# Context and x loaded with 64 consecutive rows per partition, strips transposed at a step of 64 words, l worked out group by group

## The chip, the cores and the metric

One core of a Trainium2 chip runs the whole kernel: TensorE (PE), VectorE (DVE), ScalarE (ACT), GpSimd (POOL), and SyncE (SP), which here only issues DMAs. The metric is the device time of one execution in microseconds. Times are given as the median of several executions; one execution was also profiled.

## The reference

The kernel computes one graph attention layer over 8192 nodes with a residual and a layer norm. `adj` is 8192 x 8192 float32 of zeros and ones (268 MB), `context` 8192 x 512, `x` 8192 x 256.

```python
in_fts = context @ W_common.T
left   = in_fts @ w_left  + b_left      # l, one number per row of adj
right  = in_fts @ w_right + b_right     # r, one number per column of adj
logits = left[:, None] + right[None, :]
logits = where(logits >= 0, logits, 0.2 * logits)
logits = where(adj <= 0, -inf, logits)
h      = relu(softmax(logits, axis=-1) @ x)
out    = layernorm(x + h, axis=-1, eps=1e-5)
```

## The kernel before

The weight vectors are folded first: `v = W_common.T @ w` for both sides, replicated over all partitions in PSUM (L267), so that l and r are dot products of context rows with `v`.

**Setup.** SP loads context in 8 chunks of 2 MB, each as four DMAs of 32 partitions (L200). Partition `32q + p` takes the rows `2048q + 32j + p`: a row per piece, 2 KB. The chunks go through four buffers that lie in X, so chunk 4 and later wait for earlier dot products. DVE forms all 64 r and 24 of the l dot products (L418); the other 40 l go through a product on POOL (L249) and a sum on ACT (L305). Then come extremes of r, exponentials, and the tables: `tab` in PSUM holds for each partition quadrant the packed word of every one of its 2048 columns (L472), `arow` the word of every row (16 small copies, L476). x (8.4 MB) is loaded after that in 16 DMAs of 1 KB pieces (L212). ACT takes square sums of x (64 of L321), DVE a scale `Fx`, then ACT writes the 64 high parts of x (L326) and DVE the 64 low parts (L510) as float16 into X, which are the moving side of all later products.

**Main loop.** adj is taken in 256 strips `n` of 32 rows, 1 MB each; a strip lies in one of four buffers as 128 partitions x 2048 words, quadrant q holding columns 2048q to 2048q + 2047. Four strips make a group `g` of 128 rows; there are 64 groups. Per strip: four DMAs (L175, waiting for the transpose of the strip four earlier), ACT turns 0/1 into a mask (L351), DVE picks the word of each edge by max and min against `tab` and `arow[:, n]` (L518, `masked(n)`), and DVE transposes 32 x 32 blocks into T (L562, `transposed(n)`). T has two halves, so the first transpose of group g waits for the products of group g - 2. Per group PE runs 192 matmuls of 257 columns (L291, L292 and L295 for each of 64 blocks), 12288 in all. What remains of a group (reciprocal, quotient, residual, norm, store) is small and trails two groups behind.

**Order.** All engines run programs written out by hand, with semaphores. The block that is transposed for product `jb` is the set of columns `2048q + 32 jb + i`, 32 consecutive words of the strip in each quadrant, which has to match the row of x that partition `32q + i` holds in X:

```python
nc.vector.transpose(T[:, o, :, k * B:(k + 1) * B],
                    strip[:, b, :].rearrange("p (j i) -> p j i", i=B)).then_inc(s_t, 1)
```

A second path for a wide range of exponents (`general_steps`) exists in both kernels and is not taken with these inputs.

Of the kernel before, what the change touches and what calls it, by code (L numbers as in the profile page):

```python
# [11 lines left out]
AX = mybir.AxisListType  # L12

# [9 lines left out]
def build(nc, x, adj, ctx_in, w_common, w_left, b_left, w_right, b_right, out):  # L23
# [16 lines left out]
    NX = 4  # L40
    XC = JB // NX
    HB = JB // 2
    OWN = [j for j in range(JB) if j % 8 in (0, 3, 6)]
# [13 lines left out]
    with stack:  # L57
# [14 lines left out]
        LR = sb("LR", [P, 2, JB])  # L72
        E = sb("E", [P, 2, JB])
        Et = sb("Et", [P, 2, JB])
        word = sb("word", [P, 2, JB])
        gen = sb("gen", [P, 2, JB])
        F = sb("F", [P, JB])
        Fx = sb("Fx", [P, JB])
        SS = sb("SS", [P, JB])
        wcol = sb("wcol", [P, 2, HID // P])  # L80
        bias = sb("bias", [P, 2])
        small = sb("small", [P, 64])
        y = xs2[:, 0:NY, :]
        xrow = xs2[:, NY:NY + 2, :]

# [4 lines left out]
        word16 = word[:, :, :].rearrange("p c j -> p (c j)").bitcast(F16).rearrange("p (c j e) -> p c j e", c=2, e=2)  # L90
        cstage = [Xflat[:, s * CT * CIN:(s + 1) * CT * CIN].rearrange("p (t k) -> p t k", k=CIN) for s in range(4)]
        xs1 = T[:, 1, :, :].rearrange("p j m -> p (j m)").rearrange("p (j d) -> p j d", d=D)
        W = strip[:, 3, 0:2 * CIN].rearrange("p (h k) -> p h k", h=2)
        wrep = strip[:, 3, 2 * CIN:2 * CIN + 4 * P].rearrange("p (c h m) -> p c h m", c=2, h=2)
        vl = strip[:, 2, 0:CIN]
        prod = strip[:, 2, CIN:3 * CIN].rearrange("p (b k) -> p b k", b=2)

        def xrows(j):
            return xs1[:, j, :] if j < HB else xs2[:, j - HB, :]
# [10 lines left out]
        mxc, diag = small[0:3, 28:29], small[0:3, 29:32]  # L110

# [4 lines left out]
        pt = stack.enter_context(nc.psum_tensor("pt", [P, 512], F32))  # L116
        tab = stack.enter_context(nc.psum_tensor("tab", [P, NQ], F32))
# [5 lines left out]
        s_ctx = [sem(f"context_in{s}") for s in range(4)]  # L123
# [3 lines left out]
        s_vl = sem("v_left_copied")  # L127
        s_prod = sem("product_ready")
        s_sum = sem("product_summed")
        s_dot = sem("dots_done")  # L130
        s_lr = sem("left_right_ready")
# [14 lines left out]
        s_xl = sem("x_low_ready")  # L146
        s_one_col = sem("ones_column_steps")
# [23 lines left out]
        def _(sp):  # L171
# [14 lines left out]

            sp.dma_start(W, w_common.rearrange("(p h) k -> p h k", p=P)).then_inc(s_w, 16)
            for c, v in enumerate((w_right, w_left)):
                sp.dma_start(wcol[:, c, :], v.rearrange("(p h) -> p h", p=P)).then_inc(s_w, 16)
            for c, v in enumerate((b_right, b_left)):  # L190
                sp.dma_start(bias[:, c:c + 1], v.broadcast_to([P, 1])).then_inc(s_w, 16)
            for c in range(NCH):
                if c >= 4:
                    end = (c - 3) * CT
                    own = sum(j < end for j in OWN)
                    sp.wait_ge(s_dot, end + own)
                    sp.wait_ge(s_prod, end - own)
# [4 lines left out]
            for n in range(2):  # L202
                load_strip(n)
            sp.wait_ge(s_sum, JB - len(OWN))
            sp.wait_ge(s_v, 1)
            for n in range(2, NB):
                load_strip(n)
            for c in range(NX):
                dst = (xs1, xs2)[c // (NX // 2)][:, c % (NX // 2) * XC:(c % (NX // 2) + 1) * XC, :]
                for q in (0, 2, 1, 3):  # L210
                    r0 = q * NQ + c * XC * B
                    sp.dma_start(dst[q * B:(q + 1) * B, :, :],  # L212
                                 x[r0:r0 + XC * B, :].rearrange("(j p) d -> p j d", p=B)).then_inc(s_x[c], 16)
            sp.wait_ge(s_xh, JB)
            sp.wait_ge(s_xl, JB)
            for g in range(2):
                load_xrow(g)
            for n in range(NS):
                g, k = divmod(n, SG)
                if n + NB < NS:  # L220
                    sp.wait_ge(s_t, n + 1)
                    load_strip(n + NB)
                if k == 2 and g >= 2:
                    load_xrow(g)
                if k == 2 and g >= 3:
                    store(g - 3)
# [6 lines left out]
        def _(pool):  # L233
# [6 lines left out]
            pool.wait_ge(s_vl, 1)  # L240
            m = 0
            for c in range(NCH):
                pool.wait_ge(s_ctx[c % 4], 64 * (c // 4 + 1))
                for t in range(CT):
                    if c * CT + t in OWN:
                        continue
                    if m >= 2:
                        pool.wait_ge(s_sum, m - 1)
                    nc.gpsimd.tensor_tensor(prod[:, m % 2, :], cstage[c % 4][:, t, :], vl, ALU.mult).then_inc(s_prod, 1)  # L249
                    m += 1  # L250
# [11 lines left out]
        def _(pe):  # L262
            pe.wait_ge(s_w, 80)
            pe.wait_ge(s_wrep, 1)
            for c in range(2):
# [16 lines left out]
            for g in range(NG):  # L282
                o = g % 2
                pe.wait_ge(s_t, (g + 1) * SG)
                if g >= 2:
                    pe.wait_ge(s_y, g - 1)
# [354 lines left out]
```

## Time and profile before

| | |
|---|---|
| median of 3 runs | 1564.39 us (1547.11 to 1564.72) |
| the profiled execution | 1557.17 us |
| its span | 1555.3 us |
| PE busy / DVE busy / ACT busy | 89% / 82% / 44% |
| mean granted clock of PE | 0.947 |

The span is the stretch that the trace covers, and the execution's own time is 1.9 us longer. PE's matmuls overlap one another in the record (a mean of 273 ns each, while a new one starts every 111 ns), so its busy time tells when it works, not how well.

### The profile page before, as it was taken

The numbers are of one execution on the slowest core, as the hardware profiler recorded it, in microseconds if no ns is written. First come the engines' busy times: TensorE is split into PE (matmuls) and PEld (weight loads), VectorE is DVE, ScalarE is ACT, GpSimd is POOL, SyncE is SP. The second block draws the span as 40 slices with busy tenths as digits, with TensorE's granted clock in tenths as the row PEclk, the third lists the DMA queues.
The fourth block names the chain that finished last, engine by engine and source line by source line (L and its number), as shares of the span: only waits on it lengthen the run. The fifth ranks groups of instructions, "written<-read, shape, count | busy, mean of one in ns | idle before, by whom it ended". The sixth has DMA issues, their size and how long they took to land.

```text
span 1555.3 us, 28279 instructions
## 1 busy us (share of the span) xinstructions
PE 1379.9 (89%) x12302; PEld 1199.8 (77%) x12302; DVE 1269.4 (82%) x1000; ACT 685.9 (44%) x852; POOL 110.2 (7%) x240
## 2 busy tenths in 40 slices
PE   1002379999999999999999999999999999999998
PEld 0002268888888888888888888888888888888887
DVE  4883698898888988888988888888889888889881
ACT  2458544444444444444444444444444444444440
POOL 4710000000000000000000000000000000000000
PEclk7555789999999999999999999999999999999999
DMA  9994598888888888888888888888888888888870
GB/s 212 270 200 87 139 220 208 221 206 207 211 208 216 213 205 211 206 207 224 203 210 210 208 210 220 205 207 211 209 218 211 205 212 208 207 223 204 208 177 12
DMA packets 85584, 312.82 MB, mean 201 GB/s; under 512 B 19792, under 2 KB 44368, under 8 KB 52688
## 3 DMA queue, kind: packets, MB, share of 16 engines
q1 hardware_dynamic: 85456, 310.98, 81.2%
q8 instruction: 96, 1.57, 0.5%
q14 instruction: 32, 0.26, 0.1%
HBM read 302.52 MB, written 8.39 MB: 200 GB/s over the span
## 4 chain that ended last, share of the span: by engine, by line
PE 87%; DMA 5%; SPq 4%; DVE 3%; ACT 1%; POOL 0%; issue 0%; POOLq 0%; DVEq 0%
PE ps L295 29%; PE ps L291 29%; PE ps L292 29%; DMA X<-in_L_gnn_context_dram 3%; SPq L212 2%; DVE X L510 2%; DMA xs<-in_x_dram 1%; SPq L200 1%; DMA strip<-in_adj_dram 1%; ACT pt L321 1%; SPq L175 1%; DVE gw L418 0%; DVE strip L518 0%; DVE T L562 0%; POOL strip L249 0%
## 5 line engine op out<-in xcount | busy, mean ns | idle before, releaser
L291 PE MATMUL ps<-X,T 128*128 128x257 f16 x4096 | 1117.3, 273 | 34.5 <-DVE T L562 32.8
L295 PE MATMUL ps<-X,T 128*128 128x257 f16 x4096 | 1125.2, 275 | 0.0
L292 PE MATMUL ps<-X,T 128*128 128x257 f16 x4096 | 1114.8, 272 | 0.0
L562 DVE STREAM_TRANSPOSE T<-strip 128x2048 f32<-128x2048 f32 x256 | 589.4, 2303 | 174.8 <-PE ps L295 174.8
L351 ACT ACTIVATE strip<-strip 128x2048 f32<-128x2048 f32 x256 | 488.8, 1910 | 413.7 <-DMA strip<-in_adj_dram 413.4
L518 DVE SCALAR_TENSOR_TENSOR strip<-tab,arow,strip 128x2048 f32<-128x2048 f32 x256 | 595.1, 2325 | 17.3 <-ACT strip L351 17.0
L291 PEld LDWEIGHTS ps<-X,T 128*128 128x128 f16 x4096 | 403.5, 99 | 85.0 <-DVE T L562 33.0
L292 PEld LDWEIGHTS ps<-X,T 128*128 128x128 f16 x4096 | 399.0, 97 | 61.3
L295 PEld LDWEIGHTS ps<-X,T 128*128 128x128 f16 x4096 | 397.2, 97 | 63.2 <-DVE X L510 7.5
L332 ACT ACTIVATE xs<-ps,small 128x256 f32<-128x256 f32 x64 | 30.4, 475 | 219.9 <-DVE small L567 219.9
L255 POOL TENSOR_SCALAR small<-small 128x1 f32<-128x1 f32 x64 | 12.3, 192 | 1398.9 <-ACT pt L340 1398.9
L336 ACT ACTIVATE small<-small 128x1 f32<-128x1 f32 x64 | 13.0, 203 | 156.2 <-DVE xs L572 156.2
L418 DVE SCALAR_TENSOR_TENSOR gw<-X,ps 128x512 f32<-128x512 f32 x88 | 54.2, 683 | 20.7 <-DMA X<-in_L_gnn_context_dram 20.7
L273 PE MATMUL pt<-ident,small 128*2 128x128 f32 x1 | 0.4, 372 | 69.0 <-DVE small L433 69.0
L273 PEld LDWEIGHTS pt<-ident,small 128*2 128x2 f32 x1 | 0.1, 80 | 70.1 <-issue 70.1
L249 POOL TENSOR_TENSOR strip<-X,strip 128x512 f32<-128x512 f32 x40 | 49.6, 1273 | 32.5 <-DMA X<-in_L_gnn_context_dram 32.5
L277 PE MATMUL pt<-ident,small 128*1 128x128 f32 x1 | 0.4, 372 | 55.5 <-DVE small L489 55.5
L277 PEld LDWEIGHTS pt<-ident,small 128*1 128x1 f32 x1 | 0.1, 79 | 55.6 <-DVE small L489 55.6
L305 ACT ACTIVATE strip<-strip 128x512 f32<-128x512 f32 x40 | 25.2, 630 | 38.8 <-POOL strip L249 38.8
L345 ACT ACTIVATE xs<-xs,small 128x256 f32<-128x256 f32 x64 | 37.5, 586 | 3.6 <-POOL small L259 3.6
L257 POOL TENSOR_TENSOR small<-small 128x1 f32<-128x1 f32 x64 | 35.2, 551 | 5.3
L340 ACT ACTIVATE pt<-xs,small 128x256 f32<-128x256 f32 x64 | 30.6, 478 | 2.1
(71 smaller groups left out, 198.3 us busy)
## 6 DMA issues: line engine op xcount, KB each, us to landing
strip<-in_adj_dram SPq DMA_DIRECT2D x1024, 256.0 KB, 4.6
X<-in_L_gnn_context_dram SPq DMA_DIRECT2D x32, 512.0 KB, 16.9
xs<-in_x_dram SPq DMA_DIRECT2D x64, 128.0 KB, 5.0
out_dram<-xs SPq DMA_DIRECT2D x64, 128.0 KB, 4.9
T<-in_x_dram SPq DMA_DIRECT2D x8, 512.0 KB, 13.9
xs<-in_x_dram SPq DMA_DIRECT2D x8, 512.0 KB, 14.1
strip<-in_L_gnn_W_common_dram SPq DMA_DIRECT2D x1, 512.0 KB, 3.6
wcol<-in_L_gnn_w_right_dram SPq DMA_DIRECT2D x1, 1.0 KB, 3.3
```

The lines of the kernel that those rows point to most:

```text
L212: sp.dma_start(dst[q * B:(q + 1) * B, :, :], x[r0:r0 + XC * B, :].rearrange("(j p) d -> p j d", p=B)).then_inc(s_x[c], 16)
L249: nc.gpsimd.tensor_tensor(prod[:, m % 2, :], cstage[c % 4][:, t, :], vl, ALU.mult).then_inc(s_prod, 1)
L257: nc.gpsimd.tensor_tensor(st(5, o), st(4, o), power, ALU.pow).then_inc(s_rstd, 1)
L291: nc.tensor.matmul(ps[o][:, 0:D + 1], hi, X16[:, jb, 0:D + 1], start=(jb == 0), stop=False)
L292: nc.tensor.matmul(ps[o][:, 0:D + 1], lo, X16[:, jb, 0:D + 1], start=False, stop=False)
L295: m = nc.tensor.matmul(ps[o][:, 0:D + 1], hi, X16[:, jb, D + 2:2 * D + 3], start=False, stop=(jb == JB - 1))
L345: nc.scalar.activation(y[:, o, :], y[:, o, :], ACT.Identity, scale=st(5, o), bias=st(6, o)).then_inc(s_out, 1)
L351: nc.scalar.activation(s, s, ACT.Relu, scale=KEEP).then_inc(s_m, 1)
L418: nc.vector.scalar_tensor_tensor(out=gw[:, junk * CIN:(junk + 1) * CIN], in0=cstage[c % 4][:, t, :], scalar=1.0, in1=ps[side][:, 0:CIN], o ...
L510: nc.vector.scalar_tensor_tensor(out=X16[:, j, D + 2:2 * D + 2], in0=xrows(j), scalar=Fx[:, j:j + 1], in1=X16[:, j, 0:D], op0=ALU.mult, op ...
L518: nc.vector.scalar_tensor_tensor(out=s, in0=tab[:, :], scalar=arow[:, n:n + 1], in1=s, op0=ALU.max, op1=ALU.min).then_inc(s_p, 1)
L562: nc.vector.transpose(T[:, o, :, k * B:(k + 1) * B], strip[:, b, :].rearrange("p (j i) -> p j i", i=B)).then_inc(s_t, 1)
```

## The change

Context and x are laid out so that partition p holds rows 64p to 64p + 63. Each context chunk is then one DMA over 128 partitions in pieces of 16 KB, with a home of its own (T and X), and waits for nothing; x follows in four such DMAs. Word `64i + j` of a strip's quadrant now belongs with partition `32q + i`, block j, so the transposes read the strip at a step of 64 words, and `tab` is written in that order.

In this layout DVE gets r from the 64 dot products, but not l in the order of the rows of adj. For l, 512 context rows (1 MB) are loaded once more for each four groups (`load_left_rows`), 16.8 MB over the kernel; DVE forms four dot products (`left_dot`), spreads them by strip (`left_by_strip`), PE carries the result to all quadrants (`spread_left`), and DVE and ACT turn it into 16 words of `arow` (`left_step`, `left_exponentials`), all interleaved with the strips of the four groups before. POOL's and ACT's share of the l products is gone. The first four strips are loaded right behind x; square sums cover two rows at once (32 instructions) and run before the first masks; the 64 high parts stand between the first masks; POOL forms 24 of the low parts and DVE 40; in group 0 PE runs all products with high parts first and the 64 with low parts after them.

```diff
-                for q in (0, 2, 1, 3):
-                    rows = ctx_in[q * NQ + c * CT * B:q * NQ + (c + 1) * CT * B, :]
-                    sp.dma_start(cstage[c % 4][q * B:(q + 1) * B, :, :],
-                                 rows.rearrange("(t p) k -> p t k", p=B)).then_inc(s_ctx[c % 4], 16)
+            def load_left_rows(b):
+                rows = ctx_in[b * LB * P:(b + 1) * LB * P, :].rearrange("(g p) k -> p g k", p=P)
+                sp.dma_start(lctx0 if b == 0 else lctx, rows).then_inc(s_lc, 16)
+            def load_context(c):
+                sp.dma_start(cstage[c], ctx_in.rearrange("(p j) k -> p j k", p=P)[:, c * CT:(c + 1) * CT, :]).then_inc(
+                    s_ctx[c], 16)
...
+                if n % LW == 12 and n // LW + 2 < NLB:
+                    b = n // LW + 2
+                    sp.wait_ge(s_ld, LB * b)
+                    load_left_rows(b)
...
+            for j in range(0, NPL, XB):
+                rows = xrows(j, XB)
+                pool.wait_ge(s_xh, j + XB)
+                nc.gpsimd.tensor_tensor(rows, rows,
+                                        Fx[:, j:j + XB].rearrange("p (j c) -> p j c", c=1).broadcast_to([P, XB, D]),
+                                        ALU.mult).then_inc(s_xf, 1)
+                pool.wait_ge(s_xf, j // XB + 1)
+                nc.gpsimd.tensor_tensor(X16[:, j:j + XB, D + 2:2 * D + 2], rows, X16[:, j:j + XB, 0:D],
+                                        ALU.subtract).then_inc(s_xp, XB)
...
+            def spread_left(b):
+                pe.wait_ge(s_lm, b + 1)
+                if b >= 2:
+                    pe.wait_ge(s_la, 3 * (b - 1))
+                nc.tensor.matmul(pt[:, 0:LW], R[:, :, :].rearrange("p q i -> p (q i)"),
+                                 L[:, :, :].rearrange("p g s -> p (g s)"), start=True, stop=True).then_inc(s_lb, 1)
...
+                if g % LB == 1 and g // LB + 1 < NLB:
+                    spread_left(g // LB + 1)
...
+            for j in range(HB):
+                if 2 * j % XC == 0:
+                    act.wait_ge(s_x[2 * j // XC], 16)
+                if j >= 1:
+                    act.wait_ge(s_ss, j)
+                nc.scalar.activation(ps[1][:, 0:2 * D], xrows(2 * j, 2).rearrange("p j d -> p (j d)"), ACT.Square,
+                                     accum_out=SS[:, j:j + 1]).then_inc(s_ss, 1)
...
-            nc.vector.transpose(tab[:, :].rearrange("p (j c) -> p j c", c=B),
+            nc.vector.transpose(tab[:, :].rearrange("p (c j) -> p j c", c=B),
...
                 nc.vector.transpose(T[:, o, :, k * B:(k + 1) * B],
-                                    strip[:, b, :].rearrange("p (j i) -> p j i", i=B)).then_inc(s_t, 1)
+                                    strip[:, b, :].rearrange("p (i j) -> p j i", i=B)).then_inc(s_t, 1)
```

The new helper that DVE runs between strips (b is the block of four groups ahead, k the strip within the present one):

```python
def left_step(b, k):
    if 7 <= k < 7 + LB:
        q = k - 7
        if q == 0:
            dve.wait_ge(s_lc, (b + 1) * 16)
        dve.wait_ge(s_ld, b * LB + q - 1)
        left_dot(b, q, lctx, ljunk[:, q % 2, :])
    if k == 11:
        left_by_strip(b)
    if k == 13:
        ...   # three instructions on 16 columns
    if k == 14:
        ...   # waits for ACT's exponentials, then five on 16 columns
```

DVE's program in the main loop, before: the end of a group, and the first strips of the next. L518 is the mask step, L562 the transpose, L567 and L572 finish an older group.

```order
L518 SCALAR_TENSOR_TENSOR strip<-tab,arow,strip 128x2048 [waits mask_or_exponentials_ready]
L562 STREAM_TRANSPOSE T<-strip 128x64x32 [waits words_masked,products_done]
L567 RECIPROCAL small<-ps 128x1 [waits products_done]
L518 SCALAR_TENSOR_TENSOR strip<-tab,arow,strip 128x2048 [waits mask_or_exponentials_ready]
L562 STREAM_TRANSPOSE T<-strip 128x64x32 [waits words_masked]
L572 SCALAR_TENSOR_TENSOR xs,small<-xs,small 128x256 [waits xrow_in0,quotient_ready]
```

The same place in the changed kernel, at the last group of a block (L622 is the mask step, L666 the transpose).

```order
L666 STREAM_TRANSPOSE T<-strip 128x64x32 [waits words_masked]
L599 TENSOR_SCALAR E<-pt,small 128x16 [waits left_on_all_quadrants]
L600 TENSOR_SCALAR gen<-pt,small 128x16
L602 TENSOR_SCALAR E<-E,small 128x16 [waits left_exponent_steps]
L676 SCALAR_TENSOR_TENSOR xs,small<-xs,small 128x256 [waits xrow_in1,quotient_ready]
L622 SCALAR_TENSOR_TENSOR strip<-tab,arow,strip 128x2048 [waits mask_or_exponentials_ready]
L666 STREAM_TRANSPOSE T<-strip 128x64x32 [waits words_masked]
L605 TENSOR_SCALAR Et<-E 128x16 [waits left_exponentials_ready]
L608 TENSOR_TENSOR E<-E,Et 128x16 [waits left_word_steps]
L609 TENSOR_SCALAR word<-Et 128x16
L611 TENSOR_SCALAR word<-E 128x16 [waits left_word_steps]
L614 SCALAR_TENSOR_TENSOR arow<-word,small,gen 128x16 [waits left_word_steps]
```

Per four groups DVE gains four dot products, one spreading step and these eight small ones, with one new wait for PE and one for ACT.

ACT's program in the setup, before, from the end of the l sums on (L351 is the mask, L321 a square sum, L326 a high part).

```order
L309 ACTIVATE E<-E 128x128 [waits exponents_ready]
L311 ACTIVATE F<-F 128x64 [waits exponents_ready]
L351 ACTIVATE strip<-strip 128x2048 [waits adj_in0]
L321 ACTIVATE pt,SS<-T 128x256 [waits x_in0]
L321 ACTIVATE pt,SS<-xs 128x256 [waits x_square_sums,x_in2]
L326 ACTIVATE X<-T,Fx 128x256 [waits x_factors_ready]
L326 ACTIVATE X<-xs,Fx 128x256 x32
```

And in the changed kernel (L400 is the mask, L364 a square sum over two rows, L371 a high part).

```order
L356 ACTIVATE E<-E 128x80 [waits exponents_ready]
L358 ACTIVATE F<-F 128x64 [waits exponents_ready]
L364 ACTIVATE ps,SS<-xs 128x512 [waits x_in0]
L364 ACTIVATE ps,SS<-T 128x512 [waits x_square_sums,x_in2]
L400 ACTIVATE strip<-strip 128x2048 [waits adj_in0]
L371 ACTIVATE X<-xs,Fx 128x256 [waits x_factors_ready] x10
L400 ACTIVATE strip<-strip 128x2048 [waits adj_in1]
L371 ACTIVATE X<-xs,Fx 128x256 [waits x_factors_ready] x10
```

The square sums now stand ahead of the first mask, and the high parts are spread among the first four masks.

## Rows read from the trace of the kernel before

**Rows 1.** Page: busy time and share of the span.

```profile
PE 1379.9 (89%) x12302; PEld 1199.8 (77%) x12302; DVE 1269.4 (82%) x1000; ACT 685.9 (44%) x852; POOL 110.2 (7%) x240
```

**Rows 2.** Windows: busy us of each engine, granted clock, DMA share, GB/s.

```profile
120.00:140.00 20.00, 0.00 (x0) 0.00 (x0) 0.00 (x0) 17.32 (x70) 0.00 (x0) 0.50 0.68 134
180.00:200.00 20.00, 0.00 (x0) 0.00 (x0) 16.72 (x8) 8.20 (x5) 0.00 (x0) 0.50 0.96 229
300.00:600.00 300.00, 300.00 (x2702) 263.28 (x2701) 258.52 (x156) 131.44 (x127) 13.07 (x42) 1.00 0.85 210
```

**Rows 3.** Waits: engine and line, awaited, us in total, times, longest.

```profile
ACT strip L351 <- DMA strip<-in_adj_dram: 413.4, 194, 8.6
DVE T L562 <- PE ps L295: 174.8, 61, 3.0
```

**Rows 4.** Timeline of DVE in mid-loop: start, us, instruction, idle before.

```profile
717.23 2.31 DVE L562 STREAM_TRANSPOSE T<-strip 128x2048 f32<-128x2048 f32 x1 [2.96 <-PE ps L295]
719.47 0.13 DVE L567 RECIPROCAL small<-ps 128x1 f32<-128x1 f32 x1
719.52 2.32 DVE L518 SCALAR_TENSOR_TENSOR strip<-tab,arow,strip 128x2048 f32<-128x2048 f32 x1
721.76 2.30 DVE L562 STREAM_TRANSPOSE T<-strip 128x2048 f32<-128x2048 f32 x1
...
738.57 2.31 DVE L562 STREAM_TRANSPOSE T<-strip 128x2048 f32<-128x2048 f32 x1 [2.96 <-PE ps L295]
```

**Rows 5.** Timeline of the setup: start, us, instruction.

```profile
84.04 0.25 DVE L426 TENSOR_SCALAR LR<-LR,bias 128x64 f32<-128x64 f32 x1
...
96.21 2.35 DVE L518 SCALAR_TENSOR_TENSOR strip<-tab,arow,strip 128x2048 f32<-128x2048 f32 x1 [0.26 <-issue]
...
144.35 12.89 ACT L326 ACTIVATE X<-T,Fx 128x256 f16<-128x256 f32 x32 [2.59 <-DVE Fx L504]
...
203.73 0.39 PE L291 MATMUL ps<-X,T 128*128 128x257 f16 x1 [32.85 <-DVE T L562]
```

**Rows 6.** Chain that ended last, in the setup: start, us, what.

```profile
26.94 3.14 DVE gw L418 x10
...
83.50 0.73 ACT strip L305 x2
...
140.72 0.52 ACT pt L321 x2
...
142.81 0.59 PE pt L279 x2
...
144.97 25.59 DVE X L510 x64
...
176.92 11.32 DMA strip<-in_adj_dram
```

**Rows 7.** Windows of the DMA in the setup, columns as in rows 2.

```profile
2.00:6.00 4.00, 0.00 (x0) 0.00 (x0) 0.00 (x0) 0.00 (x0) 0.00 (x0) 1.00 0.49 155
...
66.00:70.00 4.00, 0.00 (x0) 0.00 (x0) 3.21 (x11) 1.61 (x6) 2.62 (x3) 0.50 1.05 302
...
180.00:184.00 4.00, 0.00 (x0) 0.00 (x0) 2.35 (x1) 1.46 (x2) 0.00 (x0) 0.50 1.00 231
```

**Rows 8.** Groups by line and shape: busy us, mean ns, idle before.

```profile
L249 POOL TENSOR_TENSOR strip<-X,strip 128x512 f32<-128x512 f32 x40 | 49.6, 1273 | 32.5 <-DMA X<-in_L_gnn_context_dram 32.5
...
L476 DVE COPY arow<-word 32x64 f32<-32x64 f32 x16 | 2.9, 184 | 0.2
L472 DVE STREAM_TRANSPOSE tab<-word 128x2048 f32<-128x2048 f32 x1 | 2.3, 2327 | 0.0
...
L482 DVE SCALAR_TENSOR_TENSOR X<-F,X 128x64 f16<-128x64 f32 x1 | 0.4, 448 | 0.0
L480 DVE TENSOR_SCALAR X<-F 128x64 f16<-128x64 f32 x1 | 0.3, 320 | 0.0
...
L465 DVE TENSOR_SCALAR word<-Et 128x128 f16<-128x128 f32 x1 | 0.2, 234 | 0.0
```

More of the change, by code:

```diff
@@ L40, in build @@
     NX = 4
+    LB = 4
+    NLB = NG // LB
+    LW = LB * SG
+    NPL = 24
     XC = JB // NX
     HB = JB // 2
-    OWN = [j for j in range(JB) if j % 8 in (0, 3, 6)]
     WSCALE = 2.0 ** 10
@@ L218, in _ @@
+            for c in range(NX):
+                if c == NX // 2:
+                    sp.wait_ge(s_dot, 2 * CT)
+                sp.dma_start(xrows(c * XC, XC), x.rearrange("(p j) d -> p j d", p=P)[:, c * XC:(c + 1) * XC, :]).then_inc(
+                    s_x[c], 16)
+            sp.wait_ge(s_v, 2)
+            for n in range(NB):
+                load_strip(n)
             for n in range(NS):
@@ L312, in _, with high_part @@
             act.wait_ge(s_set, 4)
             general = act.value_load(flag.bitcast(I32)[0:1, 0:1])
[L315 to L323 removed]
+            def high_part(j):
@@ L324, in high_parts, with left_exponentials @@
                 act.wait_ge(s_Fx, 1)
-                for j in range(JB):
-                    nc.scalar.activation(X16[:, j, 0:D], xrows(j), ACT.Copy, scale=Fx[:, j:j + 1]).then_inc(s_xh, 1)
+                nc.scalar.activation(X16[:, j, 0:D], xrows(j), ACT.Copy, scale=Fx[:, j:j + 1]).then_inc(s_xh, 1)
+            def left_exponentials(b):
+                act.wait_ge(s_la, b * 3)
+                nc.scalar.activation(E[:, lw], E[:, lw], ACT.Exp, scale=1.0 - SLOPE).then_inc(s_le, 1)
             def quotient(g, o, turn):
@@ L370, in general_steps @@
                         exponentials((it * NY + u) * SG + k, k % NB)
+                        if more and u * SG + k == 13:
+                            left_exponentials(it + 1)
             with act.If(general == 0):
@@ L374, in _ @@
                     keep(n)
-                square_sums()
-                high_parts()
+                    for j in range(n * 10, n * 10 + 10):
+                        high_part(j)
+                for j in range(NB * 10, JB):
+                    high_part(j)
                 for n in range(NB, NS):
@@ L388, in _ @@
             with act.Else():
-                square_sums()
-                high_parts()
+                for j in range(JB):
+                    high_part(j)
                 general_steps(0)
                 general_steps(1)
-                with act.Fori(2, NG // NY) as it:
+                with act.Fori(2, NG // NY - 1) as it:
                     general_steps(it)
+                general_steps(NG // NY - 1, more=False)
             for g in range(NG - 2, NG):
@@ L579, in finish, with general_steps @@
                     residual(g, o, turn)
-            def general_steps(it):
+            def general_steps(it, more=True):
                 for u in range(NY):
```

335 lines of the change are left out of this document (188 added, 147 removed).

## Prediction

> **What bounds the kernel now.** I read the page's busy shares first, then the windows, then the waits. PE is busy for 89% of the span and nothing else comes near it except DVE with 82% [rows 1], so the question is where PE is bound by itself and where it waits. The windows answer it: from 300 us on every 300 us hold 2702 matmuls without a gap at the full clock [rows 2], one each 111 ns. 192 of them make a group, 21.3 us, and the timeline of DVE shows the same step, 717.23 to 738.57 [rows 4]. The waits show what is left on the others: DVE waits for PE 61 times, 174.8 us in total, 2.87 us per group; ACT waits for adj DMAs 413.4 us [rows 3]. So in the loop PE sets the time, DVE has 2.87 of 21.3 us to spare, and DMA is busy for 85% [rows 2]. Only what happens before PE's unbroken run can be saved. That run begins at 203.73 us with group 1 [rows 5], and 1351.6 us later the span ends, which is 63 groups plus a short tail. The first 204 us are a chain: DMA of context, then of x, ACT's square sums, high and low parts, and then the wait for strips that could not be fetched before (11.32 us of DMA at 176.92) [rows 6].
>
> **The setup.** I rebuild the chain of the changed kernel from these rows.
> Context: 0.5 MB of weights, 16.8 MB and the first 1 MB for l, with no wait between. The rate isn't shown for such loads in bulk. The nearest rows are 155 GB/s at a DMA share of 0.49 while the weights came in (the one large load over 128 partitions), 316 GB/s if scaled to a full share; 302 for context at its fastest; 231 for strips [rows 7]. I take 302: last chunk at 2 + 61 = 63 us. DVE needs 0.63 us per dot product (10 records in 3.14 us) [rows 6], 8 after the last chunk: 68 us, against 84.04 now [rows 5].
> Tables: 12.2 us from there to the first mask now [rows 5]; the 16 copies (2.9 us) [rows 8] become one. They end near 78 and nobody waits: ACT needs only the exponents, some 4 us after the dot products.
> x: 8.4 MB more at 302 GB/s, 91 us. Square sums over 512 words: 0.73 us for the two records of such an ACT step, 0.52 us for 256 words [rows 6]; 32 of them take 24 us instead of 35, from 72 to 96, and the last chunk of x leaves 6 us after 91. Both give 97. The scale takes 2.6 us, the idle time in front of L326 [rows 5]: 99.
> Strips 0 to 3 land between 94 and 105, just behind x, and no longer hold anything up. The second four are fetched during what follows, which removes the 11.32 us.
> Then ACT: 30 high parts at 0.403 us (12.89 us for 32) [rows 5] and three masks at 1.9 between them bring the mask of strip 3 to 117. DVE's mask step and transpose follow (4.5 us, from the starts 719.52 and 721.76 and the next step) [rows 4]: 121.5. 40 low parts at 0.40 (25.59 us for 64) [rows 6]: 137.5. Eight steps for strips 4 to 7 at 2.23: PE begins group 1 at 155. POOL's 12 instructions on 1024 words, twice 1273 ns each [rows 8], end near 130 and are covered by DVE's low parts. That cover is 8 us deep; beyond it each us counts only for group 0, which has another 18 us.
> Sum: 203.7 - 155 = 48 us earlier.
> Bounds: at 231 GB/s everything moves back by 27 us (21 us gained). With a DMA faster than DVE, 68 dot products of 0.63 us set the pace and the start is at 143 (61 us gained).
> POOL may also get in the way of DVE. In this trace POOL never works beside a DVE instruction with two SBUF inputs; the low parts are such. The overlap is 10 us, so the price lies between 0 and 10 us; I take 0. The Trainium skill, page "SBUF — State Buffer", section "Who interferes with whom", calls the port pair of the two an exclusive lock; by it the price would be near the 10 us, and no row here shows it.
>
> **The loop.** DVE's additions per four groups: four dot products (2.5 us), nine small instructions that I price like L465, 0.23 us [rows 8], so 4.6 us, 1.15 per group. DVE goes from 18.5 to 19.6 us in 21.3: hidden, and 1.7 us per group, 0.43 per transpose, are left as cover.
> PE's additions: 15 products of a 128 x 128 float32 weight with 16 columns. The nearest is L279, 0.59 us for two records [rows 6]; I take 0.5 each, 7 us in all, on the path; bounds 0 and 9. They wait for a DVE step that comes before the last transposes of a later group, about 3 us before PE gets there.
> DMA: 15 more MB in 1344 us raise the share from 0.85 to about 0.9. Each MB takes 4.5 us at 231 GB/s in front of one strip. A strip's path (issue, landing, mask) has a few us to spare, and DVE's lateness is made up from the 1.7 us per group. I take 0; if every one were paid, 63 us.
> ACT: one more exponential per four groups, ACT is half idle. DVE waits for it at strip 14 of 16, behind ACT's mask of strip 16; that is at hand about when DVE comes. Queued behind this wait is DVE's next mask step. 0, up to 1.7 us per group without effect.
>
> **The transposes.** 252 of them stand in the loop, 2.30 us each for 2048 words at a step of one [rows 4]. Now they read at a step of 64 words. No row shows a wide read step alone. Two rows write float16 at a step of 1032 bytes: L480 takes 320 ns for 64 elements where L465 takes 234 for 128, so a wide write is dear. L482 reads one stream and writes at that step, 448 ns, 128 ns more than L480, or 2.0 ns per element; but it is another operation, with two inputs, and reads from the place where it writes [rows 8]. By it a transpose could cost up to 4.1 us more. For a transpose itself there is one other reading pattern: L472 reads each word 32 times in succession and takes 2327 ns, against 2303 for contiguous words. Fetching 32 times fewer words makes it no faster: the pace is one element per cycle of DVE, not the fetch, and the output is written in runs of 32 words in either kernel. I take 0, the value of the nearest row in kind, and keep 4.1 us as the other end.
> The Trainium skill says otherwise: "Advanced Engine Details and Errata", section "Memory Cachelines", has SBUF lines of 16 bytes and wants at least two hits on a line to absorb the latency; a step of 256 bytes hits each line once. It gives no figure; the rival below has it as a doubling. The step from L480 to L482 speaks for it, L472 is silent on it.
>
> **Sum.** 1557.2 (the profiled execution, 1.9 above its span) - 48 + 7 = 1516 us. The median of the runs is 7 us above the profiled one; I forecast 1520 us. The bounds of rate, POOL and PE give 1500 to 1550.
>
> **Rivals.**
> (A) The strided reads cost DVE two cycles per element, 2.13 us more per transpose. DVE then needs 19.6 + 8.5 = 28.1 us per group, more than PE: 63 x 28.1 from about 140, plus PE's last group and the tail (27 us), 1940 us. It decides from 2.9 us per transpose: 0.43 are covered, and each 0.1 above costs 25 us, so the 41 us are gone at 0.16 more. For it: L482, and that DVE has little to spare. Against it: L472 and L562 alike. Chance 0.18. At the far end (4.1 us more) it would be 2.4 ms; that is included.
> (B) A part of that, a transpose of 2.9 to 3.4 us: 1545 to 1680 us. Chance 0.09.
> (C) The gain is given back: context at the rate of the strips (27 us), POOL in DVE's way (10), late strips behind the l rows (some of the 63), so that PE shows gaps once in four groups. 1535 to 1580. For it: the DMA share of 0.85 and ACT's waits on strips. Against: DVE's spare time. Chance 0.13.
> (D) Loads over 128 partitions run so fast that DVE sets the pace of the setup: 1490 to 1505. The row with 316 GB/s at a scaled share speaks for it. Chance 0.05.
>
> **How the numbers follow.** The forecast has 0.55. A difference under 2%, 1533 to 1596 us, is about what a measurement can't tell from none (the three runs spread over 1.1%). Faster by over 2%: 0.50 of the forecast and D, 0.55. Within 2%: 0.05 of the forecast, 0.12 of C and 0.01 of B, 0.18. Slower: A, 0.08 of B and 0.01 of C, 0.27. The range has to hold 8 in 10: it leaves out A and the lowest end of D, and takes in B: 1495 to 1680. The forecast's own range is 1500 to 1550.
>
> **What would show it.** In the profile of the changed kernel: L666 at 2.3 us (A: 4.4), with waits on PE of some 1.7 us per group; PE's unbroken run from about 155 us, 2702 matmuls per 300 us less those for l; the last context chunk by 63 us; square sums done by 97; 40 low parts on DVE at 0.40 us beside POOL's. I am wrong if DVE shows no wait for PE in the loop and PE waits for L666 in every group (A, B), if PE's gaps come every fourth group (C), or if x lands later than 100 us.

## The result, and the profile after

The changed kernel takes 1728.9 us (median of 4; 1728.4 to 1730.5) against 1563.7 us before: a ratio of 1.106, 95% interval 1.104 to 1.109. The forecast was 1520 us, range 1495 to 1680: a gain was forecast and a loss came.

The page of the changed kernel, the rows that answer to [rows 1], and its costliest groups on DVE (columns as in [rows 8]):

```profile
PE 1435.1 (83%) x12334; PEld 1225.6 (71%) x12334; DVE 1659.2 (96%) x1181; ACT 645.9 (37%) x722; POOL 84.3 (5%) x212
...
L666 DVE STREAM_TRANSPOSE T<-strip 128x2048 f32<-128x2048 f32 x256 | 951.1, 3716 | 0.0
...
L622 DVE SCALAR_TENSOR_TENSOR strip<-tab,arow,strip 128x2048 f32<-128x2048 f32 x256 | 599.0, 2340 | 4.3 <-ACT strip L400 3.7
```

DVE has gone from 82% to 96% and PE from 89% to 83%. Mask steps cost what they did; a transpose has gone from 2.3 to 3.7 us, and the idle time in front of it from 174.8 us [rows 3] to zero. DVE is the bound. The windows say the same as a count: 300 us used to hold 2702 matmuls [rows 2], now 2330. PE's granted clock is 0.95 in this window, against 1.00 before, now that PE has gaps; DVE is busy in 299.36 of the 300 us, so the clock of PE sets nothing here.

```profile
300.00:600.00 300.00, 272.48 (x2330) 232.39 (x2329) 299.36 (x184) 112.35 (x112) 11.15 (x36) 0.95 0.77 191
```

The waits have turned round. In [rows 3] DVE waited for PE; now PE waits for DVE, at the first product of a group (L336) and at the small product that spreads l (L307). The lines give the us in total, how often, and the longest:

```profile
ACT strip L400 <- DMA strip<-in_adj_dram: 503.8, 147, 19.5
...
PE ps L336 <- DVE T L666: 134.0, 49, 28.3
...
PE pt L307 <- DVE L L476: 92.6, 16, 20.7
```

DVE's timeline in mid-loop gives the step of four groups, from one L605 to the next (start, us, instruction):

```profile
702.01 0.13 DVE L605 TENSOR_SCALAR Et<-E 128x16 int32<-128x16 int32 x1
...
702.86 2.35 DVE L622 SCALAR_TENSOR_TENSOR strip<-tab,arow,strip 128x2048 f32<-128x2048 f32 x1
705.13 3.68 DVE L666 STREAM_TRANSPOSE T<-strip 128x2048 f32<-128x2048 f32 x1
708.72 2.32 DVE L622 SCALAR_TENSOR_TENSOR strip<-tab,arow,strip 128x2048 f32<-128x2048 f32 x1
...
801.58 0.13 DVE L605 TENSOR_SCALAR Et<-E 128x16 int32<-128x16 int32 x1
```

99.57 us for four groups, 24.9 us per group, where PE alone sets 21.3 [rows 4]. No idle time stands in front of any of these rows. The mask step of strip 4 starts at 132.67 us; 63 groups of 24.9 us from there, and 26 us for PE's last group and the tail, make 1727, the span.

The setup did become short. DMA moved 431 GB/s from 20 to 40 us and 389 from 40 to 60, more than any row before showed; DVE's dot products waited twice at the start, 7.5 us in all, and then followed one another; the last ended at 58.3 us, and PE began group 1 at 158.24 us instead of 203.73 [rows 5].

```profile
20.00:40.00 20.00, 0.58 (x2) 0.50 (x2) 17.74 (x54) 0.00 (x0) 0.00 (x0) 0.50 1.01 431
...
158.24 0.40 PE L336 MATMUL ps<-X,T 128*128 128x257 f16 x1 [18.55 <-DVE T L666]
```

### The profile page after: what moved, and what is told of

Read it like the earlier page. It is cut to its first block, busy times and chain, and to the rows that moved or that the text cites. A ratio compares the mean times of both kernels' runs of the same rounds, so it can differ in the third digit from the quotient of the medians.

```text
span 1727.0 us, 28390 instructions
## 1 busy us (share of the span) xinstructions
PE 1435.1 (83%) x12334; PEld 1225.6 (71%) x12334; DVE 1659.2 (96%) x1181; ACT 645.9 (37%) x722; POOL 84.3 (5%) x212
## 4 chain that ended last, share of the span: by engine, by line
DVE 71%; issue 24%; ACT 2%; PE 1%; DMA 1%; SPq 0%; POOL 0%; POOLq 0%; ACTq 0%; DVEq 0%
DVE strip L622 33%; DVE T L666 30%; DVE xs L471 2%; DVE tab L488 2%; DVE xs L676 1%; ACT ps L364 1%; DMA T<-in_L_gnn_context_dram 1%; DVE X L583 1%; PE ps L336 0%; PE ps L339 0%; PE ps L337 0%; DVE small L671 0%; ACT X L371 0%; DVE arow L614 0%; DVE gen L600 0%
## 5 line engine op out<-in xcount | busy, mean ns | idle before, releaser
L336 PE MATMUL ps<-X,T 128*128 128x257 f16 x4096 | 1135.0, 278 | 134.0 <-DVE T L666 134.0
L337 PE MATMUL ps<-X,T 128*128 128x257 f16 x4096 | 1132.1, 277 | 0.0
L339 PE MATMUL ps<-X,T 128*128 128x257 f16 x4032 | 1125.7, 279 | 0.0
L666 DVE STREAM_TRANSPOSE T<-strip 128x2048 f32<-128x2048 f32 x256 | 951.1, 3716 | 0.0
L400 ACT ACTIVATE strip<-strip 128x2048 f32<-128x2048 f32 x256 | 488.2, 1908 | 505.5 <-DMA strip<-in_adj_dram 503.8
L622 DVE SCALAR_TENSOR_TENSOR strip<-tab,arow,strip 128x2048 f32<-128x2048 f32 x256 | 599.0, 2340 | 4.3 <-ACT strip L400 3.7
L336 PEld LDWEIGHTS ps<-X,T 128*128 128x128 f16 x4096 | 413.0, 101 | 204.8 <-DVE T L666 119.2
L337 PEld LDWEIGHTS ps<-X,T 128*128 128x128 f16 x4096 | 406.1, 99 | 66.9
L339 PEld LDWEIGHTS ps<-X,T 128*128 128x128 f16 x4032 | 398.1, 99 | 61.9
L307 PE MATMUL pt<-L,R 128*128 128x16 f32 x32 | 9.1, 365 | 92.6 <-DVE L L476 92.6
L307 PEld LDWEIGHTS pt<-L,R 128*128 128x128 f32 x32 | 7.5, 289 | 97.6 <-DVE L L476 76.1
L471 DVE SCALAR_TENSOR_TENSOR xs<-xs,vl 128x512 f32<-128x512 f32 x60 | 39.1, 652 | 0.0
L394 ACT ACTIVATE xs<-xs,small 128x256 f32<-128x256 f32 x64 | 37.5, 586 | 3.6 <-POOL small L292 3.6
L389 ACT ACTIVATE xs<-xs,small 128x256 f32<-128x256 f32 x64 | 32.6, 509 | 2.1
L676 DVE SCALAR_TENSOR_TENSOR xs<-xs,small 128x256 f32<-128x256 f32 x64 | 30.0, 469 | 1.3 <-ACT xs L381 1.1
L671 DVE RECIPROCAL small<-ps 128x1 f32<-128x1 f32 x64 | 9.2, 144 | 20.5 <-PE ps L339 20.5
L488 DVE SCALAR_TENSOR_TENSOR tab<-T,ps 128x512 f32<-128x512 f32 x32 | 20.9, 726 | 7.5 <-DMA T<-in_L_gnn_context_dram 7.5
```

Of the source, the lines that this page charges most:

```text
L336: nc.tensor.matmul(ps[o][:, 0:D + 1], hi, X16[:, jb, 0:D + 1], start=(jb == 0), stop=False)
L337: nc.tensor.matmul(ps[o][:, 0:D + 1], lo, X16[:, jb, 0:D + 1], start=False, stop=False)
L339: m = nc.tensor.matmul(ps[o][:, 0:D + 1], hi, X16[:, jb, D + 2:2 * D + 3], start=False, stop=(jb == JB - 1))
L389: nc.scalar.activation(junk_row, y[:, o, :], ACT.Square, bias=st(2, o), accum_out=st(3, o)).then_inc(s_var, 1)
L394: nc.scalar.activation(y[:, o, :], y[:, o, :], ACT.Identity, scale=st(5, o), bias=st(6, o)).then_inc(s_out, 1)
L400: nc.scalar.activation(s, s, ACT.Relu, scale=KEEP).then_inc(s_m, 1)
```

## The experiments

Two theories stood at first. **S**: the step of 64 words alone makes DVE the bound. **L**: the work for l, put into the loop, is a large part of it. Later runs ask what the step costs and where, what made the setup short, and whether the gain can be had without the price. Where an edit leaves columns or rows matched otherwise than in the reference, the expectation says so; of such a run only the time and the trace are used.

### One line back: contiguous reads

```diff
-                                    strip[:, b, :].rearrange("p (i j) -> p j i", i=B)).then_inc(s_t, 1)
+                                    strip[:, b, :].rearrange("p (j i) -> p j i", i=B)).then_inc(s_t, 1)
```

> The changed kernel with one line back: the transposes read 32 consecutive words again (the table and the layout stay, so columns are matched wrongly and the output is not the reference's). Theory S, the step of 64 words alone makes the loop slow: transposes 2.3 us instead of 3.7, DVE below PE again (19.6 us of 21.3 per group), PE without gaps, 1512 us. Theory L, the l steps in the loop (DVE's dot products, PE's waits for them) are a large part: transposes 2.3 us, but gaps of PE stay and the time is above 1560 us.

Measured: 1508.5 us (1507.7 to 1508.7), 0.965 of the kernel before (0.9635 to 0.9667). S holds, L falls: with all of the l work in the loop PE runs without gaps. A window of this run, its transposes, and then DVE's largest waits:

```profile
300.00:600.00 300.00, 300.00 (x2705) 263.37 (x2703) 271.84 (x215) 131.34 (x129) 13.08 (x42) 1.00 0.89 221
```

```profile
L666 DVE STREAM_TRANSPOSE T<-strip 128x2048 f32<-128x2048 f32 x256 | 589.1, 2302 | 79.7 <-PE ps L339 79.7
```

```profile
DVE T L666 <- PE ps L339: 79.7, 47, 3.0
DVE strip L622 <- ACT strip L400: 46.4, 23, 3.7
```

DVE is left with 126.1 us of waiting, 2.0 us per group. That is the cover of this loop: the work that DVE can take on before PE has to wait for it. The one line costs 220 us.

### The same line in the kernel before

```diff
-                                    strip[:, b, :].rearrange("p (j i) -> p j i", i=B)).then_inc(s_t, 1)
+                                    strip[:, b, :].rearrange("p (i j) -> p j i", i=B)).then_inc(s_t, 1)
```

> The kernel before with one line changed: the transposes read at a step of 64 words (columns are matched wrongly, the output is not the reference's). Nothing of the l steps is in it. Theory S: DVE needs 18.5 + 4 x 1.4 = 24.2 us per group, 63 groups from about 188 us and PE's last group: 1740 us. Theory L: the transposes alone cost less than DVE has spare, under 1600 us.

Measured: 1723.9 us (1721.5 to 1724.6), a ratio of 1.103. Its transposes take 3707 ns, and 2402 matmuls stand in the 300 us from 300 on.

```profile
L562 DVE STREAM_TRANSPOSE T<-strip 128x2048 f32<-128x2048 f32 x256 | 948.7, 3707 | 0.0
```

So the step is sufficient by itself, in either setup.

### How much of it is covered

```diff
+                view = "p (i j) -> p j i" if k in (0,) else "p (j i) -> p j i"
                 nc.vector.transpose(T[:, o, :, k * B:(k + 1) * B],
-                                    strip[:, b, :].rearrange("p (j i) -> p j i", i=B)).then_inc(s_t, 1)
+                                    strip[:, b, :].rearrange(view, i=B)).then_inc(s_t, 1)
```

(the second run has `k in (0, 2)`; both start from the run with contiguous reads)

> As the run with contiguous reads (1508.5 us), but the first of the four transposes of each group reads at a step of 64 words (output not the reference's). If DVE's spare time is a true cover, one such transpose (1.43 us) fits into what DVE has left in that run (waits of 79.7 + 46.4 us, 2.0 us per group): at most 1515 us. If any delay of DVE reaches PE, 63 x 1.43 = 90 us more, 1598 us.

> As before, with the first and third transpose of each group at a step of 64 words: 2.86 us per group against 2.0 of cover, so 0.86 x 63 = 54 us more than 1508.5: 1562 us by the cover; 1688 us if nothing is covered.

Measured: 1510.3 us and 1573.5 us. The transposes of the two runs:

```profile
L667 DVE STREAM_TRANSPOSE T<-strip 128x2048 f32<-128x2048 f32 x256 | 683.3, 2670 | 8.5 <-PE ps L339 8.5
```

```profile
L667 DVE STREAM_TRANSPOSE T<-strip 128x2048 f32<-128x2048 f32 x256 | 776.7, 3035 | 0.0
```

One wide transpose per group, 94 us of DVE's work in all (683.3 against 589.1), costs 2 us; two cost 65 us, four cost 220. That is a cover with an edge near 2 us per group. The second came out 11 us above the expectation. Some 5 of them are the price, 1.47 us per wide transpose here (776.7 against 589.1, 128 of them wide) in place of 1.43. For the rest, DVE still waits 15.9 us for ACT's masks there, so it may be that not all of its spare time can be used; that was not tried by itself.

### Steps by themselves

A kernel with no other work, run once: DVE instructions on 2048 words, four of each, one after the other.

> No part of the computation: 2048-word transposes, masks and copies on DVE by themselves, each four times, at steps of 1, 2, 4, 8, 16, 32, 64 words and in rows padded to 65, 68, 72 and 96 words, to and from PSUM, and a wide write step; ACT copies at steps 1 and 64. If the cost is one of 16-byte lines, steps 1 and 2 take 2.3 us and 4 and above 3.7. If it is a bank conflict, step 64 costs more than 65 or 68. If it belongs to reading and writing SBUF at once, a step-64 transpose into PSUM takes 2.3 us. If every strided read of DVE pays, the mask and the copy at a step of 64 take 1.4 us more too.

DVE's timeline; the lines are, in order, transposes at steps of 1, 2, 4, 64 and 65 words, at 64 words into PSUM, at 64 words out of PSUM, at 64 words on the side that is written, and the mask operation contiguous and with a read at 64 words:

```profile
15.40 9.35 DVE L61 STREAM_TRANSPOSE dst<-src 128x2048 f32<-128x2048 f32 x4
24.78 9.35 DVE L64 STREAM_TRANSPOSE dst<-src 128x2048 f32<-128x2048 f32 x4
34.17 15.35 DVE L67 STREAM_TRANSPOSE dst<-src 128x2048 f32<-128x2048 f32 x4
...
94.24 14.60 DVE L79 STREAM_TRANSPOSE dst<-src 128x2048 f32<-128x2048 f32 x4
108.88 15.40 DVE L85 STREAM_TRANSPOSE dst<-src 128x2048 f32<-128x2048 f32 x4
...
184.38 14.55 DVE L101 STREAM_TRANSPOSE pm<-src 128x2048 f32<-128x2048 f32 x4
198.97 9.37 DVE L105 STREAM_TRANSPOSE dst<-pm 128x2048 f32<-128x2048 f32 x4
208.37 14.62 DVE L108 STREAM_TRANSPOSE wide<-src 128x2048 f32<-128x2048 f32 x4
223.02 9.27 DVE L112 SCALAR_TENSOR_TENSOR flat<-pm,src 128x2048 f32<-128x2048 f32 x4
232.32 14.53 DVE L116 SCALAR_TENSOR_TENSOR flat<-pm,src 128x2048 f32<-128x2048 f32 x4
```

A step of two words is free. From four words on the price is nearly the same, 1.3 to 1.5 us per 2048 words, at 4, 8, 16, 32, 64, 65, 68, 72 and 96. Padding rows to 65 words does not help, so it is not a conflict that the power of two makes. It belongs to SBUF on either side and to the mask operation as well; a wide read out of PSUM costs nothing. A plain copy of 2048 words goes from 1.25 to 1.92 us. ACT pays more: 1910 ns contiguous, 3782 at a step of 64.

### Finer steps, and the two small rows

> No part of the computation: more steps on DVE and ACT, each four times. If the limit is 16 bytes, transposes at a step of 3 words (12 bytes) take as long per block as at 1, at 4 words longer; masks on 1024 float16 words pay at a step of 8 elements (16 bytes), not at 4; float32 at 4 words, not at 2 or 3. The two small rows that the prediction read (64 elements, step 1032 bytes): near and far reads and writes apart; if wide reads cost 0.7 ns per element, the far read adds 45 ns, and the rest of the 128 ns belongs to reading and writing there at once or to the other operation. ACT: steps of 2, 4 and a wide write.

This kernel too was run once. 1024 float16 words in the mask operation take 1225 ns at a step of 4 elements and some 1.96 us at 8; float32 words 1224 ns at steps of 1 and 2, some 1.96 us at 4. Transposes of 1536 words take 2.23 us at a step of 3 words and 2.91 at 4; the contiguous rate of 2312 ns for 2048 would give 1.73. So it goes by bytes: free at 8, part of the price at 12, all of it at 16. ACT takes 1910 ns for 2048 words at a step of 1, 2.05 us at 2, 3.85 at 4, and 3.76 with the step of 64 words on the side that it writes. The small instructions on 64 elements (groups by line and shape):

```profile
L124 DVE SCALAR_TENSOR_TENSOR xw<-src,flat 128x64 f16<-128x64 f32 x4 | 1.8, 440 | 0.1
L128 DVE SCALAR_TENSOR_TENSOR xw<-src,xw 128x64 f16<-128x64 f32 x4 | 1.8, 440 | 0.1
...
L113 DVE TENSOR_SCALAR xw<-src 128x64 f16<-128x64 f32 x4 | 1.2, 311 | 0.1
...
L120 DVE SCALAR_TENSOR_TENSOR flat<-src,xw 128x64 f16<-128x64 f32 x4 | 1.1, 278 | 0.1
L116 DVE SCALAR_TENSOR_TENSOR flat<-src,flat 128x64 f16<-128x64 f32 x4 | 0.9, 224 | 0.1
L110 DVE TENSOR_SCALAR flat<-src 128x64 f16<-128x64 f32 x4 | 0.8, 196 | 0.1
```

L116 reads and writes near, L120 reads at a step of 1032 bytes, L124 writes at it, L128 does both. L110 and L113 are the operation with one input, near and with the wide write. The wide read alone adds 54 ns, 0.84 ns per element. With the wide write the read adds nothing: 440 and 440.

### What made the setup short

> The changed kernel with the layout of the kernel before (context in pieces of 2 KB and x in pieces of 1 KB, four DMAs of 32 partitions each, but still with homes of their own and no waits; contiguous transposes, table in the old order). The whole computation is done. Theory S: faster than both kernels, as far as the setup's gain holds without the 64-row layout: with 230 to 300 GB/s in the setup 1520 to 1540 us, against 1512 with the long pieces. If the layout itself is what makes the setup short: 1550 us or more.

Its edit puts back the four DMAs of 32 partitions, contiguous transposes and the old table order:

```diff
-                sp.dma_start(cstage[c], ctx_in.rearrange("(p j) k -> p j k", p=P)[:, c * CT:(c + 1) * CT, :]).then_inc(
-                    s_ctx[c], 16)
+                for q in (0, 2, 1, 3):
+                    rows = ctx_in[q * NQ + c * CT * B:q * NQ + (c + 1) * CT * B, :]
+                    sp.dma_start(cstage[c][q * B:(q + 1) * B, :, :],
+                                 rows.rearrange("(t p) k -> p t k", p=B)).then_inc(s_ctx[c], 16)
```

Measured: 1549.0 us (1548.0 to 1552.2), 0.991 (0.989 to 0.993). The loop is whole again (2705 matmuls in 300 us), but only 14 of the 55 us remain: homes of their own, no waits and the rest of the new setup are worth little when the loads run at 222 to 236 GB/s, and PE begins group 1 at 195.21 us. The missing 40 us are the rate, as the next run shows. It is not a fixed number: the profiled execution of the kernel before, with such DMAs too, moved 234, 255 and 280 GB/s in the three windows from 20 to 80 us, and the kernel before with the one line changed (the second run above), whose setup is the same, 229, 228 and 231. Why was not tried.

> As the run with contiguous reads, but context and x come in single DMAs over 128 partitions with one row per piece (2 KB and 1 KB) in place of 16 KB pieces (rows in another order, output not the reference's). It tells apart what makes the setup's loads fast. If it is the 128 partitions of one DMA, the setup stays as short: 1508 to 1515 us. If it is the length of the pieces, the loads run at 220 to 240 GB/s as in the run with the old layout: 1545 to 1552 us.

```diff
-                sp.dma_start(cstage[c], ctx_in.rearrange("(p j) k -> p j k", p=P)[:, c * CT:(c + 1) * CT, :]).then_inc(
+                sp.dma_start(cstage[c], ctx_in.rearrange("(j p) k -> p j k", p=P)[:, c * CT:(c + 1) * CT, :]).then_inc(
```

(x likewise, and the transposes are contiguous.) Measured: 1509.2 us (1508.6 to 1510.3). The pieces are as short as in the kernel before, and the time is that of the long ones. One window of each of these two runs, first with 32 partitions, then with 128:

```profile
20.00:40.00 20.00, 0.00 (x0) 0.00 (x0) 8.35 (x27) 0.00 (x0) 0.00 (x0) 0.50 1.07 236
```

```profile
20.00:40.00 20.00, 0.58 (x2) 0.50 (x2) 17.03 (x52) 0.00 (x0) 0.00 (x0) 0.50 1.05 387
```

Both have the DMA share full (1.07 and 1.05). The reach of one DMA over the partitions makes the rate, not the 64 consecutive rows. One thing changed along with the reach: a DMA is 2 MB in the fast run and 512 KB in the slow one. Two traces speak against the size. In the run with the old layout one DMA still reaches over 128 partitions, the first 1 MB for l in pieces of 2 KB; by its place in the queue it runs from about 24 to 27 us, and these are the windows there:

```profile
22.00:24.00 2.00, 0.00 (x0) 0.00 (x0) 0.00 (x0) 0.00 (x0) 0.00 (x0) 0.50 1.06 205
24.00:26.00 2.00, 0.00 (x0) 0.00 (x0) 1.54 (x5) 0.00 (x0) 0.00 (x0) 0.50 1.03 374
26.00:28.00 2.00, 0.00 (x0) 0.00 (x0) 2.00 (x7) 0.00 (x0) 0.00 (x0) 0.50 1.10 235
```

And 512 KB DMAs over 128 partitions (the run after the next) moved 105 GB/s at a DMA share of 0.26, which is 404 if scaled to a full share. A 512 KB DMA over 128 partitions that keeps all engines busy was not run.

### Versions that do the whole computation

**Two rows per piece** (a step of two words in the transposes, still 32 partitions per DMA):

> Whole computation. Layout with two consecutive rows of context and x per piece (4 KB and 2 KB), so that transposes read at a step of two words, which cost nothing in the steps run (9.35 us for four, as for a step of one). Transposes 2.3 us, loop as in the run with contiguous reads; the setup gains as far as 4 KB pieces go faster than 2 KB ones: 1525 to 1548 us.

```diff
-                                 rows.rearrange("(t p) k -> p t k", p=B)).then_inc(s_ctx[c], 16)
+                                 rows.rearrange("(t p u) k -> p t u k", p=B, u=2)).then_inc(s_ctx[c], 16)
...
-                                    strip[:, b, :].rearrange("p (j i) -> p j i", i=B)).then_inc(s_t, 1)
+                                    strip[:, b, :].rearrange("p (j i u) -> p j u i", i=B, u=2)).then_inc(s_t, 1)
```

Measured: 1550.3 us (1548.7 to 1551.5), transposes 2305 ns. The step is free in the kernel as well, and pieces of twice the length bring nothing (235, 224 and 223 GB/s from 20 to 80 us).

**The same, each DMA over all 128 partitions** as four quadrants of 32:

> Whole computation. The layout with two consecutive rows per piece (transposes at a step of two words, which cost nothing), but every DMA of context and x covers all 128 partitions: 32 DMAs of 512 KB and 32 of 256 KB in place of 32 and 16 over 32 partitions. If the reach over 128 partitions makes the setup's loads fast, as the run with short pieces says, DMA runs at 370 GB/s or more and the time is 1507 to 1520 us, faster than every version that does the whole computation. If only the large single DMAs were fast (their number, SP's issue of some 0.5 us each), 1540 us or more.

```diff
...
+                    sp.dma_start(cstage[c][:, u:u + 2, :].rearrange("p u k -> p (u k)"),
+                                 ctx_in.rearrange("(q j p u) k -> q p j (u k)", q=Q, p=B, u=2)[:, :, t, :]).then_inc(
+                                     s_ctx[c], 16)
```

Measured: 1690.7 us (1690.1 to 1691.3). A clear miss, of the setup alone: the loop has 2706 matmuls in 300 us. A window of the setup:

```profile
100.00:140.00 40.00, 0.00 (x0) 0.00 (x0) 10.59 (x32) 0.00 (x0) 0.00 (x0) 0.50 0.26 105
```

A DMA share of 0.26 is four of sixteen engines, and the outermost dimension of the source is now the four quadrants. The Trainium skill, page "DMA: Bandwidth & Descriptors", section "Rules for kernel authors", says that an outermost dimension of c < 16 confines the whole DMA to at most c engines; the trace agrees, with 105 GB/s.

**Two queues.** The two-row version with 32 partitions per DMA; SP issues quadrants 0 and 1, ACT quadrants 2 and 3.

> Whole computation. The layout with two consecutive rows per piece, in DMAs over 32 partitions that spread over all DMA engines, as in the run that gave 1550 us; but ACT, which has nothing to do in the setup, issues those of quadrants 2 and 3 while SP issues 0 and 1. If the 220 to 236 GB/s come from one DMA of 32 partitions at a time being served, with two queues two quadrants are written at once and the rate is 380 GB/s or more: 1508 to 1520 us. If a DMA over 32 partitions is slow whatever runs beside it, 1545 to 1555 us.

```diff
+            for c in range(NCH):
+                for q in (2, 3):
+                    rows = ctx_in[q * NQ + c * CT * B:q * NQ + (c + 1) * CT * B, :]
+                    act.dma_start(cstage[c][q * B:(q + 1) * B, :, :].rearrange("p (t u) k -> p t u k", u=2),
+                                  rows.rearrange("(t p u) k -> p t u k", p=B, u=2)).then_inc(s_ctx[c], 16)
```

Measured: 1529.4 us (1529.1 to 1530.6), 0.978 (0.976 to 0.979). Between the two expectations: the rate is 268, 304 and 306 GB/s in the three windows from 20 to 80 us, more than one queue's 235, 224 and 223 and less than 387. Half of the rate's 40 us come back.

**ACT takes the wide step.** The 64-row layout stays. ACT's mask reads the strip at the step and writes it in transposing order to another of three buffers; the first four strips are done as in the changed kernel, with the table read in the strip's order out of PSUM.

> Whole computation (the path for a wide range is kept, not taken). The 64-row layout stays, but the step of 64 words is moved from DVE's transposes to ACT's mask, which reads the strip at that step and writes it in transposing order into one of three other buffers; the first four strips are done as in the changed kernel. ACT's mask takes 3.8 us instead of 1.9 (3782 ns in the steps run), 17 us of ACT per group of 21.3; DVE back at 2.3 us per transpose. If ACT's spare time covers it: 1515 to 1530 us, faster than both kernels and than the old layout with the new setup (1549). If strips now arrive late behind ACT: DVE waits on ACT in every group and the time is above 1560.

```diff
-                nc.scalar.activation(s, s, ACT.Relu, scale=KEEP).then_inc(s_m, 1)
...
+                act.wait_ge(s_t, n - 2)
+                nc.scalar.activation(mk[n % 3].rearrange("p (j i) -> p j i", i=B),
+                                     s.rearrange("p (i j) -> p j i", i=B), ACT.Relu, scale=KEEP).then_inc(s_m, 1)
```

Measured: 1528.8 us (1522.9 to 1530.2), 0.977 (0.974 to 0.979). ACT's mask now takes 3.84 us, the transposes are back at 2301 ns, and DVE waits 122 us for ACT.

```profile
L408 ACT ACTIVATE xs<-strip 128x2048 f32<-128x2048 f32 x168 | 644.9, 3839 | 168.8 <-DMA strip<-in_adj_dram 155.2 <-issue 12.1 <-DVE T L687 1.1
```

Two things keep it above 1508 us: PE begins group 1 at 158.99 us instead of 152.05, and from there on it has ten gaps, 13 us in all. So two versions that compute everything take 2.2 to 2.3% less than the kernel before; what the layout promised, 3.5%, none of them reached.

## Why the prediction was wrong

**The transposes.** "I take 0, the value of the nearest row in kind, and keep 4.1 us as the other end" is the step that failed. The term is 1.4 us (3716 against 2302 ns). The kind was wrong: L472 reads each word 32 times in succession, and so stays on the same bytes; that shows what an easy pattern costs, and it was read as if it showed that fetching is free. The other end came from L482 minus L480, 2.0 ns per element; the small runs show that this difference is that of the two operations (the read adds 0 ns beside a wide write), while a wide read by itself adds 0.84 ns per element, and 0.69 in the kernel's transposes of 2048. L480 was the row to go by, though it shows the other side: it is a wide write, and wide accesses of SBUF cost DVE about as much in either direction.

The rule that I set against it, in "Advanced Engine Details and Errata" of the Trainium skill, section "Memory Cachelines", was right: it asks for at least two hits on a line of 16 bytes. The runs agree, with steps of 8 bytes free and steps of 16 not. My doubling of it, two cycles per element, was too much for DVE (3.7 us, not 4.4) and is right for ACT (3782 against 1910 ns).

**The cover.** 0.43 us per transpose was nearly right: the run with contiguous reads leaves 2.0 us per group, 0.50 each. Past it nearly everything is paid: 4 x 1.43 - 2.0 = 3.7 us per group, 234 us over 63 groups, of which 220 were measured. With 1.43 in place of 0 the sum of the prediction would have been 1520 + 252 x 1.0 = 1772 us, 2.5% above the result.

**The setup, loop and PE terms** held as a sum, with errors that cancelled in part. The run with contiguous reads took 1508.5 us where 1520 stood, and its group 1 began at 152.05 us against 155. DMA was faster than the bounds of the rows (427 GB/s from 20 to 40 us, against 302), so rival D's condition came true, and the scale of x was ready at 89.8 us instead of 99. Some 6 of these us were lost again: from the end of strip 3's mask to the first low part it took 6.7 us, not 4.5; the low parts took 17.8, not 16; and nine steps of 2.23 us stand before group 1, not eight. So the total ended 3.5 us above D's range. The whole loop, with the small products for l in it, took 1354.6 us from group 1 to the end against 1351.6, where 7 us stood for the products. Loads for l took nothing visible at a DMA share of 0.89; the prediction's bound for them is a slip, since 15 loads at 4.5 us make 68, not 63.

**POOL beside DVE** was put at 0. In the changed kernel POOL's work and DVE's low parts never met, because the slow transposes held DVE back until POOL was done:

```profile
114.13 2.14 POOL L282 TENSOR_TENSOR X<-xs,X 128x1024 f16<-128x1024 f32 x1
...
116.77 3.20 DVE L583 SCALAR_TENSOR_TENSOR X<-xs,Fx,X 128x256 f16<-128x256 f32 x8
```

In the run with contiguous reads DVE comes to its low parts earlier, and POOL's last instruction stands beside them (two lines of the timeline, then the low parts' shortest, middle and longest time in ns):

```profile
113.99 5.12 DVE L583 SCALAR_TENSOR_TENSOR X<-xs,Fx,X 128x256 f16<-128x256 f32 x8
114.33 2.13 POOL L282 TENSOR_TENSOR X<-xs,X 128x1024 f16<-128x1024 f32 x1
```

```profile
L583 DVE SCALAR_TENSOR_TENSOR X<-xs,Fx,X x8: 472/473/2348, 114.0 to 118.6; 128x256 f16<-128x256 f32 x8
```

The same eight low parts take 5.12 us instead of 3.20, and all of that is in one: it starts at 114.39 us, just after POOL's instruction, takes 2348 ns, and ends 0.3 us after it. Five other runs in which the low parts begin beside POOL's last instruction show 5.12 to 5.14 us as well. So the price was not 0 but 1.9 us, and it was small only because the two programs overlap by 2.5 us and not by 10. The Trainium skill calls the port pair that DVE and GpSimd share an exclusive lock (page "SBUF — State Buffer", section "Who interferes with whom"); these traces agree.

**The rivals.** B had the right mechanism, but its range ended at 3.4 us, a factor of 1.5, and the chip took 1.6. (Its lower end should have been 1559 us for a transpose of 2.9 us by the prediction's own terms, not 1545.) With A and B at 0.27 together the loss was foreseen as possible, at too low a chance: both rows with a wide step in them were dear, and that should have weighed more than a row without one.

## What to carry to other kernels

Before an access pattern is changed on an engine that is busy for over 80%, take the step in bytes: in these runs up to 8 bytes from one element to the next in SBUF were free for DVE, from 16 on its transposes and mask operations took 1.6 times as long (a copy, tried at 256 bytes, 1.5 times) and ACT's operations twice as long; a wide read of PSUM by DVE's transpose cost nothing. A change that trades a one-time gain (55 us here) for a price per step is to be summed as price minus cover, times the number of steps. Load rate was bought here by spreading one DMA over all partitions with an outermost dimension that splits over all engines; longer pieces gave up to 11% more rate (431 against 387 GB/s) and no time. A row without the pattern in question can't price that pattern, however near it seems.

## What was not expected of the hardware

- Pieces of 1 to 2 KB over 128 partitions move 369 to 387 GB/s in the context's windows, pieces of 16 KB 389 to 431, pieces of 1, 2 or 4 KB over 32 partitions 217 to 236 in the runs with the new setup and up to 280 in the kernel before, all with a DMA share of 0.93 or more.
- The price of a step hardly changes from 16 to 384 bytes (1.3 to 1.5 us per 2048 words), and a step of 12 bytes pays a part.
- A wide step on the side that DVE writes costs as much as one on the side that it reads (14.62 and 14.60 us for four).
- One POOL instruction of 2.13 us can hold up a DVE instruction with two SBUF inputs that starts just after it for all of its length (2348 ns instead of 473).
- Why a wide write of 64 float16 elements adds 216 ns in one operation and 115 in another was not tried.
